# Scatter-adding an expert layer's results into two sums instead of three

## The reference

```python
x = L0_attn_x                                     # (8, 512, 256)
x = _layernorm(x + attention(x, w_qkv, w_out))    # 16 heads of 16, causal softmax
x = _layernorm(x + ffn(x, ...))

def ffn(x):                                       # 4096 tokens
    probs = softmax(xf @ gate_w.T)                # 16 experts
    _, idx = top_k(probs + gate_b, 6)             # 6 experts for each token
    for e in range(16):                           # cw is 0 where e isn't chosen
        h = silu(xf @ W1.T + B1) * (xf @ W3.T + B3)        # 176 wide
        y += cw[:, e] * (h @ W2.T + B2)
    z = silu(xf @ ws1.T + bs1) * (xf @ ws3.T + bs3) @ ws2.T + bs2   # 352 wide
    return y + z
```

## Time and profile before

| what | value |
|---|---|
| median of 3 runs | 1085.8 us |
| lowest, highest | 1080.98, 1086.66 us |
| span of the profiled execution | 1081.8 us (its own time is not given beside it; the span lies inside the range of the runs) |
| mean granted TensorE clock | 0.966 of full |
| TensorE busy | 992.7 us (92%) |
| VectorE busy | 810.6 us (75%) |
| GpSimd busy | 752.6 us (70%) |
| ScalarE busy | 733.6 us (68%) |
| HBM read, written | 73.68 MB, 78.17 MB |

### The profile page before, as it was taken

One profiled execution on the slowest core, in us unless ns is written; L12 is line 12 of the kernel. 1 busy time (PEld: TensorE's weight loads), 2 busy tenths in 40 slices (PEclk: granted clock), 3 DMA queues, 4 the chain that ended last, 5 costly groups with the idle time before them and its releaser, 6 DMA issues.

```text
span 1081.8 us, 27903 instructions
## 1 busy us (share of the span) xinstructions
PE 992.7 (92%) x7478; PEld 790.0 (73%) x7479; DVE 810.6 (75%) x2622; ACT 733.6 (68%) x1859; POOL 752.6 (70%) x677
## 2 busy tenths in 40 slices
PE   8999999999999997888799999999999999999872
PEld 4546555555565654458798899999999999999872
DVE  8786878788888887747866677777777777777596
ACT  4567676666766665656455688878888888888545
POOL 4234458788888888777653677777777777777576
PEclk9899999999999999869899999999999999999985
DMA  6634254555555555457688888888887888888793
GB/s 186 175 104 118 73 155 138 181 156 179 164 172 171 167 153 189 144 171 236 204 252 220 207 137 132 132 133 131 132 130 129 137 132 132 132 134 178 190 382 128
DMA packets 134404, 176.26 MB, mean 163 GB/s; under 512 B 19328, under 2 KB 111536, under 8 KB 134064
## 3 DMA queue, kind: packets, MB, share of 16 engines
q1 hardware_dynamic: 88016, 105.83, 33.0%
q0 software_dynamic: 39024, 54.29, 29.2%
q10 hardware_dynamic: 7280, 15.11, 4.5%
HBM read 73.68 MB, written 78.17 MB: 140 GB/s over the span
## 4 chain that ended last, share of the span: by engine, by line
PE 67%; DVE 15%; ACT 6%; issue 5%; DMA 3%; POOL 2%; ACTq 1%; SPq 0%; POOLq 0%; DVEq 0%
PE psum L1099 17%; PE psum L828 10%; PE psum L1126 6%; PE psum L873 6%; PE psum L861 5%; DVE rowmax L1602 4%; PE psum L1129 4%; PE psum L842 4%; PE psum L1082 4%; PE psum L1112 2%; ACT probs L1222 2%; PE psum L1113 2%; PE psum L848 1%; DMA z_d<-y_sb,tokens 1%; DVE x1p L1618 1%
## 5 line engine op out<-in xcount | busy, mean ns | idle before, releaser
L1222 ACT ACTIVATE probs<-psum 128x512 f32<-128x512 f32 (+2 forms) x384 | 186.4, 530 | 117.5 <-PE psum L861 115.5
L1602 DVE TENSOR_REDUCE rowmax<-psum 128x1 f32<-128x512 f32 (+3 forms) x352 | 211.9, 632 | 55.6 <-PE psum L848 53.0
L2157 POOL DMA_INDIRECT xs_d<-x1p,index x192 | 204.4, 1065 | 57.8 <-issue 40.3
L1099 PE MATMUL psum<-we_hi_lo,xb_hi 128*128 x828 | 207.1, 332 | 0.0
L2229 POOL DMA_INDIRECT x_d<-y_sb,tokens x69 | 108.5, 1572 | 54.8 <-issue 31.7
L1952 DVE TENSOR_TENSOR hb<-psum,hb 128x176 f32<-128x176 f32 x207 | 70.6, 341 | 101.4 <-ACT hb L1399 97.8
L2069 POOL TENSOR_SCALAR_AFFINE_SELECT probs<-probs 128x512 f32<-128x512 f32 x128 | 88.1, 689 | 78.7 <-ACT probs L1222 76.5
L1099 PEld LDWEIGHTS psum<-we_hi_lo,xb_hi 128*128 128x128 f32 x828 | 136.9, 188 | 3.1 <-issue 0.2
L842 PE MATMUL psum<-stack_k,stack_q 96*128 96x256 bf16 (+3 forms) x512 | 129.4, 311 | 8.0 <-DVE rowmax L1602 3.4
L2229 POOL DMA_INDIRECT z_d<-y_sb,tokens x69 | 107.9, 1563 | 38.9 <-issue 25.7
L861 PE MATMUL psum<-stack_q,stack_k 99*128 99x256 bf16 (+3 forms) x512 | 119.2, 308 | 17.1 <-ACT probs L1222 14.8
(11 more groups left out here) (227 smaller groups left out, 2537.3 us busy)
## 6 DMA issues: line engine op xcount, KB each, us to landing
xb<-xs_d SPq DMA_DIRECT2D x207, 138.0 KB
stack_q<-q_h SPq DMA_DIRECT2D x48, 128.0 KB
stack_k<-k_h SPq DMA_DIRECT2D x45, 128.0 KB
w_raw<-in_we SPq DMA_DIRECT2D x9, 608.0 KB
xT_raw<-in_xT SPq DMA_DIRECT2D x9, 512.0 KB, 4.6
stack_q<-q_m SPq DMA_DIRECT2D x32, 128.0 KB
stack_k<-k_m SPq DMA_DIRECT2D x32, 128.0 KB
x_res<-in_x SPq DMA_DIRECT2D x8, 512.0 KB, 4.2
```

Of the source, the lines that this page charges most:

```text
L1099: last = nc.tensor.matmul(uv, (xb_hi, xb_lo)[a][k % 2][:, d, :], w_flat[:, bass.ds(at + b * W_COLS + d * UP, UP)], start=False, stop=d == ...
L1222: nc.scalar.activation(probs[kt][:, heads[0]:heads[0] + n, :], st[f % ST_BANKS][:, 0:n * width].rearrange("p (h t) -> p h t", h=n), ACT.Ex ...
L1602: nc.vector.reduce_max(rowmax[gpar][:, heads[0]:heads[0] + n, qt], src, AX.X).then_inc(sm_free, 1)
L2157: nc.gpsimd.indirect_dma_start(out=xs_d[:, :], out_offset=bass.IndirectOffsetOnAxis(ap=index[tp][:, n:n + 1], axis=0), in_=x1p[tp][:, n // ...
```

## The change

`SUMS` goes from 3 to 2. The results of even blocks go into `x1_d`, those of odd blocks into `z_d`, and block k's DMA waits for the landing of block k-2's. `y_d`, its clearing, its loads, its semaphores and VectorE's add of it at the end are gone. Behind the loop VectorE makes the low halves of all tiles, GpSimd none. `x1T_late` moves in front of `fin_x` in the on-chip memory.

```diff
-SUMS = 3
+SUMS = 2
...
-FINAL_FROM = DVE_LOW_UP_TO = T1 + 6
+FINAL_FROM = T1 + 6
...
-        y_d = nc.dram_tensor("y_d", (T_ALL + P, D), fp32).ap()
...
+        x1T_late = [sb(f"x1T_late{n}", [P, KD, HT_TOK]) for n in range(HALVES - HC1 - 1)]
         fin_x = [sb(f"fin_x{n}", [P, HALF, D]) for n in range(HALVES)]
         fin_z = [sb(f"fin_z{n}", [P, HALF, D]) for n in range(HALVES)]
-        fin_y = [sb(f"fin_y{n}", [P, HALF, D]) for n in range(HALVES)]
-        x1T_late = [sb(f"x1T_late{n}", [P, KD, HT_TOK]) for n in range(HALVES - HC1 - 1)]
...
-            def set_third_sum(piece):
-                rows = y_d[Y_ROWS * piece:min(Y_ROWS * piece + Y_ROWS, T_ALL + P)]
-                sp.dma_start(rows.rearrange("(q p) d -> p q d", p=P),
-                             pad_block[:, 0:D].unsqueeze(1).to_broadcast([P, rows.shape[0] // P, D])).then_inc(y_set, 16)
...
-                if b < Y_PIECES:
-                    set_third_sum(b)
...
-                sp.wait_ge(y_set, 16 * Y_PIECES)
+                sp.wait_ge(pad_stored, 16)
+                sp.wait_ge(pads_set, 16)
...
-            for n, src, dst in ((0, x1_d, fin_x), (1, z_d, fin_z), (2, y_d, fin_y)):
+            for n, src, dst in ((0, x1_d, fin_x), (1, z_d, fin_z)):
...
-                load_final(i, y_d, fin_y)
...
                 dve.wait_ge(fin_sum, m + 1)
-                dve.wait_ge(fin_third_loaded[i], 16)
-                nc.vector.tensor_tensor(fin_x[i][:], fin_x[i][:], fin_y[i][:], ALU.add).then_inc(fin_third, 1)
-                dve.wait_ge(fin_third, m + 1)
...
-                if T - 1 < DVE_LOW_UP_TO:
+                if T - 1 < T_SH:
                     low(T - 1)
...
-                else:
-                    pool.wait_ge(y_set, 16 * Y_PIECES)
                 settle(pool, passed_pool)
                 nc.gpsimd.indirect_dma_start(
-                    out=(x1_d, z_d, y_d)[k % SUMS][:, :], ...
+                    out=(x1_d, z_d)[k % SUMS][:, :], ...
...
-            for T in range(DVE_LOW_UP_TO, FINAL_FROM + HALVES):
+            for T in range(FINAL_FROM, FINAL_FROM + HALVES):
                 m = T - FINAL_FROM
-                if T < T_SH:
-                    low(T)
```

More of the change, by code:

```diff
@@ L191 @@
 NORMALIZED_BEHIND = 6
-FINAL_FROM = DVE_LOW_UP_TO = T1 + 6
+FINAL_FROM = T1 + 6
 SPLIT_FIRST_X1_AT = (3, 4)
 CLEARED, CONSTS = 11, 14
-Y_PIECES = B - 1
-Y_ROWS = P * -(-(T_ALL + P) // (P * Y_PIECES))
 GAP, GAP2 = 352, 3160
@@ L515, in postln_layer @@
         added = [sem(f"added{n}") for n in range(SUMS)]
-        y_set = sem("y_set")
         seeded = sem("seeded")
@@ L523, in postln_layer @@
         fin_loaded = [sem(f"fin_loaded{n}") for n in range(HALVES)]
-        fin_third_loaded = [sem(f"fin_third_loaded{n}") for n in range(HALVES)]
         fin_sum = sem("fin_sum")
-        fin_third = sem("fin_third")
         fin_stats_done = sem("fin_stats_done")
@@ L763, in load_final @@
             def load_final(i, src, dst):
-                sp.dma_start(dst[i][:], rows_of(src, i)).then_inc((fin_third_loaded if src is y_d else fin_loaded)[i], 16)
+                sp.dma_start(dst[i][:], rows_of(src, i)).then_inc(fin_loaded[i], 16)
             def store_final(k):
@@ L2199, in _ @@
                 iteration(b, b % 2)
[L2201 to L2205, removed]
             def bias_rows():
@@ L2225, in add_rows @@
                         pool.wait_ge(z_stored[n], 16 * (HC1 // 2))
-                else:
-                    pool.wait_ge(y_set, 16 * Y_PIECES)
                 settle(pool, passed_pool)
                 nc.gpsimd.indirect_dma_start(
-                    out=(x1_d, z_d, y_d)[k % SUMS][:, :], out_offset=bass.IndirectOffsetOnAxis(ap=tokens[:, k:k + 1], axis=0),
+                    out=(x1_d, z_d)[k % SUMS][:, :], out_offset=bass.IndirectOffsetOnAxis(ap=tokens[:, k:k + 1], axis=0),
                     in_=y_sb[k % 4][:], in_offset=None, compute_op=ALU.add).then_inc(added[k % SUMS], 16)
```

## The result

The changed kernel takes 1130.8 us (median of 4 runs, 1128.28 to 1137.61) against 1084.1 us before (median of 4, 1080.98 to 1086.66): 1.046 times as long, 95% interval 1.043 to 1.050. Forecast were 1134 us and a range of 1110 to 1158. The profiled execution took 1130.93 us with a span of 1129.2.

The account below looks back on a forecast made before the run. The prediction took TensorE to bound the loop and VectorE to be fullest in the end. First 24 blocks +12, calm loop with burst +47, end -11 made +48 on 1085.8, so 1133.8 us; range 1110 to 1158.

Parts of the forecast that it names:

- the calm loop: Blocks 24 to 206: from 2.069 to 2.30 us per block, 376.5 to 423.6 us with the burst, +47 us.
- the burst: Near block 190: the last weights' loads stretch the round trip to 7.7 us, costing about 5 us.
- The round trip: Loop: R, one scatter's start to the next's earliest start into the same sum; 3.4 + 0.4 + 0.8 = 4.6 us.
- R/3 hidden and R/2 bound: Loop: three sums give 1.53 us, under TensorE's 2.03 to 2.07; two give 2.30 us and set the pace.
- The first 24 blocks: Loop's start, landings slow beside weight loads: each trip carries two blocks, not three; +12 us, ends 0 and +20.
- The end: Behind the last scatter: third adds gone, low halves taken over by VectorE, -9.2; earlier start, -2; sum -11 us.
- VectorE runs in one chain: Behind the loop: VectorE's saved work counts in full, -9.2 us (14.2 us of adds gone, 5.0 us of low halves added).
- the reason given for the earlier start: Behind the last scatter: no third load, so x_d's load, one load of each sum and one GpSimd add; -2 us.
- 4.1 and less: Rival in the loop: landing early enough, spacing stays 2.069 us, only the end changes; 1075 us; 5%, 2% for a mixture.
- 4.35: Rival in the loop: round trip shrinks as packets get less company, 2.175 us per block; +19, 1105 us; 13%.
- 4.9: Rival in the loop: round trip grows as two scatters' packets and xb's loads coincide, 2.45 us per block; 1166 us; 10%.
- The lower clock: Rival in the loop: idling TensorE drops its clock in a quarter of 182 blocks, 64 us on top; 1198 us; 6%.

## Why the prediction was right

The mechanism of the loop, which is most of the change, was right and is shown. That the total came so near (+46.8 us between the medians, +48 forecast) is in part luck: 3.7 us too little for the calm loop and the burst stand against 4.2 us that the stage ahead happened to be shorter, and in the end three errors cancel.

**The round trip** was right in sum and in its parts: 4.6 forecast, 4.59 measured with one sum, 4.57 and 4.61 between scatters of one sum in the kernel after. A scatter lands 3.8 us after its start (3.4 + 0.4 forecast), and the next starts 0.76 us later (0.8). The steps that turned it into time, R/3 hidden and R/2 bound, hold for each number of sums: 2.05 to 2.06 us per block with three and four, 2.32 with two, 4.59 with one. And with R cut by a shorter scatter, two sums give 2.06 again.

The calm spacing is 2.325 us and not 2.30. The median from one scatter to the next of its sum is 4.59 us in the kernel after too, but the mean is 4.65: 26 of 162 are above 4.8, where the kernel with one sum has 10 of 163. GpSimd's order is a reason that fits (a scatter must also follow the one before it, so a late landing in one sum delays the other); I didn't test it. Over 182 blocks the 0.025 us make 4.6 us, and the burst near block 190 cost 4.1 and not 5: +50.7 in place of +47.

**The first 24 blocks:** +13.1 against +12. In the other kernels with two sums and whole scatters they take 65.4 to 68.9 us, and with three sums 56.9 to 59.1. By all of these the loss is 6 to 13 us, about 10 in the mean; that the pair compared gave 13.1 is luck.

**The end:** -12.2 against -11, right in sum by terms that were wrong in their sizes. VectorE's first instruction of the end, and its groups there:

```profile
1082.12 0.69 DVE L1972 TENSOR_TENSOR fin_x<-psum,fin_x 128x512 f32<-128x512 f32 x1 [6.27 <-POOL fin_x L2215]
```

```profile
L1907 DVE TENSOR_TENSOR h_lo<-hidden,h_hi 128x256 fp32r<-128x256 f32 x15 | 9.6, 637 | 0.0
...
L1581 DVE TENSOR_TENSOR x1T_end<-x1T_late,x1T_end 128x512 fp32r<-128x512 f32 x2 | 2.4, 1219 | 0.0
```

It starts 9.9 us behind the last scatter and not 13.1, a gain of 3.2 for the 2 forecast. From there to the end of VectorE's last statistics are 40.3 us, where before were 49.2, a gain of 8.8 for 9.2 (both rounded; the two gains make 12.0 of the 12.2).

The experiments take the 12.2 apart in another way. Two sums in the loop with the end left as it was give -3.3 (69.1 to 65.9), the third adds and loads -8.2 (65.9 to 57.7), the low halves on VectorE -0.8 (57.7 to 56.9). Forecast were -14.2 for the third adds, +5.0 for the low halves and -2 for the start. Two steps of the prediction failed here. The first is that VectorE runs in one chain, so that its work counts in full. The chain of the end before shows other engines:

```profile
1021.46 1.45 PE psum L828 x12
...
1023.79 0.73 POOL h_lo L2204
1024.52 1.24 POOL fin_x L2240
1025.78 1.75 DVE fin_x L1985
...
1030.46 2.93 PE psum L828 x12
...
1034.67 2.14 PE psum L828 x12
...
1038.42 1.70 POOL fin_x L2240
...
1044.10 1.29 DVE fin_x L1985
```

From 1030.4 to 1044.1 us it runs over TensorE, ScalarE and GpSimd, with 0.04 us of VectorE's in it. The second is the reason given for the earlier start. The first third add did not wait for loads: GpSimd's first add stood behind a low half, which waited for TensorE's matmuls up to 1022.9. With two sums TensorE has run ahead of the scatters when the loop ends, and the start moves from 13.1 to 10.8 us behind the last scatter though the third load is still there (VectorE waits for it).

In the kernel after a low half costs 637 ns, not the 415 of the earlier trace rows. This is the part of the 9.2 that the prediction said would come back by the Trainium skill ("GPSIMD Engine Reference", Specifications: GpSimd shares its SBUF interfaces with VectorE and contends with instructions that have two SBUF inputs). The traces agree with it: the third add takes 0.68 us when it starts with no add of GpSimd's beside it and up to 1.77 us when it starts beside one.

**The stage ahead of the loop** came out 4.2 us shorter, which I had at 0. It isn't the cleared y_d. The first scatter starts at 577.1 to 580.8 us in six other kernels that clear it, and at 577.8 to 579.1 in four that don't, where the kernel after has 574.7. The four without it have the code of the kernel after up to there, so the change isn't what made it early; I take it for a spread from one execution to the next.

**Where the text on the new profile missed.** It said that GpSimd's idle time would be put down to a DMA; most rows name y_sb or "issue", although y_sb was ready some 4.8 us earlier. It also said that TensorE would be busy near 88%; the row has 383.49 of 399 us, 96%. A matmul of L1085 has a mean of 343 ns there, 332 before, so part of the waiting seems to be counted as busy. The weight loads, the next column of the same lines, fall from 331.11 of 342 us to 345.40 of 399, 97% to 87%, near the 88%. That is a hint, not a proof. The spacing was the safe sign, the labels were not.

One sum in the prediction slipped: +33 to +64 us on 1085.8 is 1119 to 1150, not 1117 to 1152. Nothing else rests on it.

**The rivals.** R measured at 4.59 us leaves out the rivals with 4.1 and less, 4.35 and 4.9. The lower clock did not come in the calm loop with two sums, 1.00 there. In the first blocks it did come for a short time:

```profile
596.00:606.00 10.00, 7.41 (x49) 6.13 (x48) 4.85 (x23) 4.54 (x14) 3.62 (x3) 1.00 0.74 196
606.00:616.00 10.00, 6.98 (x41) 6.49 (x40) 5.07 (x22) 4.13 (x13) 5.89 (x4) 0.81 0.66 150
616.00:626.00 10.00, 10.00 (x65) 9.64 (x65) 5.46 (x27) 5.40 (x16) 5.13 (x5) 0.85 0.83 167
```

Behind 10 us in which TensorE was busy for 7.41, the mean granted clock is 0.81 and then 0.85 of full, a mix of the two levels (2.4 and 1.2 GHz); the kernel before has 1.00 there. What it adds to the 70.3 us of the first 24 blocks was not taken apart from the slow landings. With one sum the clock is 0.78 in the mean, where TensorE idles a third of the time; that kernel is bound by the landing in any case. The Trainium skill's fit of a DMA ("DMA: Bandwidth & Descriptors", the anatomy of a SWDGE DMA), counted from the scatter's start, would by the prediction's estimate have made R 3.1 us, with no loss. The measured R of 4.59 us does not agree with this start; counted from the end of the issue it would.

## What to carry to other kernels

When several transfers rotate over n targets and each must land before its target is used again, compare the full round trip divided by n with the pace of the loop: start of issue to the last packet, to the semaphore, and from there to the next start on the issuing engine. A wait that never shows in the profile can still be the reason for a buffer; the margin is what counts, and here 1.53 us against 2.06 became 2.30. In a loop held by a latency the engines look less busy, if not always by much (TensorE still read 96%), and the named releaser may be a neighbour: a change of one slot, one target or half of the size tells at once which wait is real.

## What the runs showed of the hardware

Halving the rows of an accumulating indirect DMA shortened GpSimd's issue by 10% only (1557 to 1402 ns), so a scatter of 64 rows is little cheaper to issue than one of 128. The same 128x512 add took VectorE 683 ns in one kernel and a mean of 1199 ns in another with more adds on GpSimd beside it, as a mix of 0.68 us and, when it started beside a GpSimd add, 1.55 to 1.77 us: moving work from VectorE to GpSimd kept only 1.3 us of the 6 that it should have saved. VectorE's add with an input in PSUM kept its 684 to 691 ns. By the trace's records of landed transfers the next scatter of a sum started 0.75 to 0.76 us behind the landing of the one before; the prediction had taken 0.80 from y_sb in its place.
